# Streamed heads of a fused perceiver: the average's operands exchanged, one copy for the value blocks, and a turned quotient that VectorE copies behind its subtraction

## What is computed

```python
# _L0_ffn_ref: four expert attentions, x is (64, 32, 128), h = 16, hd = 8
q = (xg @ wq[e] + bq[e]).reshape(b, s, h, hd)
k = (xg @ wk[e] + bk[e]).reshape(b, s, h, hd)
v = (xg @ wv[e] + bv[e]).reshape(b, s, h, hd)
att = jnp.einsum('bqhd,bkhd->bhqk', q, k) * sm_scale
att = jax.nn.softmax(jnp.where(validg[:, None, None, :], att, -1e9), axis=-1)
y = jnp.einsum('bhqk,bkhd->bqhd', att, v).reshape(b, s, d)
y = y @ wo[e] + bo[e]
```

## Time and profile before

| | |
|---|---|
| median of 3 runs | 2164.21 us |
| lowest and highest run | 2162.43 and 2166.15 us |
| span of the profiled execution, first to last instruction | 2160.1 us |
| busy in the span: PE, DVE, ACT, POOL | 1764.0, 1435.0, 1016.2, 915.1 us |
| mean granted TensorE clock | 0.905 |
| the three streams: `L0Ffn`, `L1Attn`, `L3Ffn` | about 406 to 636, 718 to 779 and 1931 to 2023 us |

### The profile page before, as it was taken

One profiled execution on the slowest core, in us unless ns is written; L12 is line 12 of the kernel. 1 busy time (PEld: TensorE's weight loads), 2 busy tenths in 40 slices (PEclk: granted clock), 3 DMA queues, 4 the chain that ended last, 5 costly groups with the idle time before them and its releaser, 6 DMA issues.

```text
span 2160.1 us, 50856 instructions
## 1 busy us (share of the span) xinstructions
PE 1764.0 (82%) x20448; PEld 1176.2 (54%) x20448; DVE 1435.0 (66%) x3589; ACT 1016.2 (47%) x2574; POOL 915.1 (42%) x1083
## 2 busy tenths in 40 slices
PE   6678999899878789987578789998999896457496
PEld 4324557566544556643456656666676664135286
DVE  6799995688875665447970286565767666668622
ACT  5535764566644732242322365665666651124143
POOL 2243554455540514213522333137657567433433
PEclk9878999999999989999689999999999998757588
DMA  8000000100016100071033200100000000040187
GB/s 344 1 1 0 1 1 1 75 4 5 5 54 287 59 2 1 1 286 48 2 111 113 83 26 23 30 11 20 11 25 20 6 11 1 11 169 8 39 287 237
DMA packets 60427, 130.69 MB, mean 61 GB/s; under 512 B 16713, under 2 KB 38940, under 8 KB 54560
## 3 DMA queue, kind: packets, MB, share of 16 engines
q1 hardware_dynamic: 56896, 121.32, 15.7%
q0 software_dynamic: 3296, 6.12, 0.9%
HBM read 107.97 MB, written 20.12 MB: 59 GB/s over the span
## 4 chain that ended last, share of the span: by engine, by line
PE 48%; DVE 23%; issue 14%; ACT 7%; DMA 3%; SPq 2%; POOL 2%; POOLq 0%; DVEq 0%; ACTq 0%
PE PS L3230 4%; PE PS L2517 4%; PE PS L3277 3%; PE PS L424 3%; PE PS L3261 2%; PE PS L3219 2%; PE PS L3262 2%; DMA arena<-in_ctx 2%; PE PS L460 2%; DVE arena L1808 2%; PE PS L2317 2%; PE PS L4222 2%; PE PS L4231 1%; DVE arena L253 1%; PE PS L3269 1%
## 5 line engine op out<-in xcount | busy, mean ns | idle before, releaser
L321 POOL TENSOR_TENSOR arena<-arena 128x4 f32<-128x4 f32 (+3 forms) x109 | 118.7, 1090 | 396.5 <-DVE arena L264 260.0
L3345 ACT ACTIVATE arena<-PS,arena 128x289 f32<-128x289 f32 x256 | 128.0, 507 | 79.0 <-DVE arena L3459 78.1
L3230 PE MATMUL PS<-arena 128*128 128x289 f32 x512 | 153.4, 423 | 11.5 <-ACT arena L3345 7.5
L3459 DVE TENSOR_REDUCE arena<-PS 128x1 f32<-128x289 f32 x256 | 111.0, 453 | 75.2 <-PE PS L3230 70.0
L1872 POOL TENSOR_TENSOR arena<-arena 128x128 f32<-128x128 f32 x384 | 140.9, 405 | 43.1 <-PE PS L1735 18.9
L1258 POOL TENSOR_TENSOR arena<-arena 128x512 f32<-128x512 f32 x64 | 84.0, 1312 | 109.7 <-DVE arena L1403 109.7
L1808 DVE RECIPROCAL arena<-PS 128x128 f32<-128x128 f32 x96 | 91.6, 954 | 56.9 <-PE PS L1773 48.0
L1839 ACT COPY arena<-PS 32x128 f32<-32x128 f32 x384 | 99.7, 260 | 49.2 <-PE PS L1749 44.2
L3230 PEld LDWEIGHTS PS<-arena 128*128 128x128 f32 x512 | 87.9, 192 | 38.2 <-ACT arena L3345 19.6
L3188 POOL TENSOR_TENSOR arena<-arena 128x1024 f32<-128x1024 f32 x14 | 33.0, 2359 | 166.0 <-ACT arena L3336 166.0
L460 PE MATMUL PS<-arena 128*128 128x128 f32 (+4 forms) x576 | 84.9, 294 | 21.8 <-DVE arena L4338 7.8
(11 more groups left out here) (451 smaller groups left out, 4838.8 us busy)
## 6 DMA issues: line engine op xcount, KB each, us to landing
arena<-in_ctx SPq DMA_DIRECT2D x32, 1091.0 KB
arena<-in_f_w SPq DMA_DIRECT2D x39, 514.0 KB
arena<-in_ctx SPq DMA_DIRECT2D x16, 834.0 KB, 23.1
lists<-arena SPq DMA_DIRECT2D x8, 1040.0 KB, 10.6
arena<-in_f_w SPq DMA_DIRECT2D x32, 256.0 KB
arena<-in_ctx SPq DMA_DIRECT2D x16, 512.0 KB
arena<-in_mid SPq DMA_DIRECT2D x1, 3796.5 KB, 12.5
arena<-in_late SPq DMA_DIRECT2D x1, 3204.0 KB, 10.3
```

Source lines behind the costliest of these rows:

```text
L321: e.tensor_tensor(x, x, half.broadcast_to(list(x.shape)), ALU.pow).then_inc(*T.done("norm_root", tag))
L3230: e.matmul(PS[:, b, 0:UL], self.qt[i % 2][:, j, P * k:P * k + P], self.kt[i % 3][:, j, :], start=True, stop=True).then_inc(*T.done("k3_sco ...
L3345: e.activation(self.weights(n, k, 0, UL), PS[:, self.score_bank(n, k), 0:UL], ACT.Exp, bias=self.st[:, h, k:k + 1], accum_out=self.st[:, h ...
L3459: e.tensor_reduce(self.st[:, n % 2, k:k + 1], PS[:, self.score_bank(n, k), 0:UL], AXX, ALU.max, negate=True).then_inc(*T.done("k3_least", ...
```

## The change

- **values.** TensorE writes each head's values into their own columns of bank 4 (block j, group n, head h), so the bank holds the blocks as they are needed and zeros elsewhere; four matmuls against a cleared tile set these zeros once for each stream, ahead of the first scores. ACT takes the whole bank in one copy of 128x512.
- **vB** is 36 columns wide a block: 32 of values and four of ones (`rowmask`), written once by POOL in place of the memsets.
- **average.** Operands are exchanged: the turned weights are the PE weights now, the value blocks are streamed (16 matmuls of 36 columns). The result has the tokens on the partitions, with the sums of the weights beside it, so the four matmuls of L1773 go.
- **divide.** The reciprocal is taken of 128x16, and the product is written to a new tile `mean`.
- **back and out.** One transpose on PE turns `mean` into columns 256 to 383 of bank 7, and DVE copies that (128x128) to `OT`. Both come one step later than the division: `back(m - 3)` right behind the scores of m, `out(m - 3)` behind the subtraction of m (in `L1Attn` behind the causal product of m-1) and ahead of the division of m-2. `h_out`, for which the average of the next tile and the output projection wait, is now the end of that copy.

```diff
-    BANK = 5
+    BANK, WIDE = 5, S + HG
...
-        self.vB = [room.take(BT * D) for _ in range(3)]
+        self.vB = [room.take(BT * NG * self.WIDE) for _ in range(3)]
...
+            own = PS[:, 4, :].rearrange("p (j n h d) -> p j h n d", j=BT, n=NG, h=HG)
             for j in range(BT):
                 for h in range(HG):
-                    k = e.matmul(PS[S * h:S * h + S, 4, S * j:S * j + S].rearrange("p (n d) -> p n d", n=NG),
+                    k = e.matmul(own[S * h:S * h + S, j, h],
                                  self.xT[:, P * i + S * j:P * i + S * j + S], wv[:, h], start=True, stop=True)
...
-            for j in range(BT):
-                for n in range(NG):
-                    r = slice(S * n, S * n + S)
-                    k = e.matmul(PS[r, 7, S * j:S * j + S], v[:, D * j + S * n:D * j + S * n + S],
-                                 p[:, P * n + S * j:P * n + S * j + S], start=True, stop=True)
             for n in range(NG):
-                k = e.matmul(PS[S * n:S * n + S, 7, P:2 * P], g.C["headsum"], p[:, P * n:P * n + P], start=True, stop=True)
+                for j in range(BT):
+                    a = NG * j + n
+                    k = e.matmul(PS[S * j:S * j + S, 7, w_ * n:w_ * n + w_], p[:, P * n + S * j:P * n + S * j + S],
+                                 v[:, w_ * a:w_ * a + w_], start=True, stop=True)
             k.then_inc(*T.done("h_average", (tag, m)))
             free[7] = ("h_out", (tag, m))
+
+        def back(m):
+            for w in T.due(("h_mean", (tag, m))):
+                e.wait_ge(*w)
+            e.transpose(PS[:, 7, 2 * P:3 * P], self.mean[m % 2], g.C["ident"]).then_inc(*T.done("h_back", (tag, m)))
+
+        for w in T.due(free[4], ("h_cleared", tag)):
+            e.wait_ge(*w)
+        for j in range(BT):
+            e.matmul(PS[:, 4, P * j:P * j + P], self.mean[0], g.C["ident"], start=True, stop=True)
 
         for m in range(self.N + 3):
             if m < self.N:
                 scores(m)
+            if 0 <= m - 3 < self.N:
+                back(m - 3)
+            if m < self.N:
                 values(m)
...
-            e.reciprocal(rest, PS[:, 7, P:2 * P]).then_inc(*T.step())
-            for w in T.due(T.prev()):
-                e.wait_ge(*w)
-            e.tensor_tensor(self.OT[:, P * i:P * i + P], PS[:, 7, 0:P], rest, ALU.mult).then_inc(*T.done("h_out", (tag, m)))
+            e.reciprocal(rest.rearrange("p (n h) -> p n h", n=NG), both[:, :, S:]).then_inc(*T.step())
...
+            e.tensor_tensor(self.mean[m % 2].rearrange("p (n h d) -> p n h d", n=NG, h=HG),
+                            both[:, :, 0:S].rearrange("p n (h d) -> p n h d", h=HG),
+                            spread(rest.rearrange("p (n h) -> p n h", n=NG), [P, NG, HG, HD], 3),
+                            ALU.mult).then_inc(*T.done("h_mean", (tag, m)))
+
+        def out(m):
+            i = m % NT
+            for w in T.due(("h_back", (tag, m))):
+                e.wait_ge(*w)
+            e.tensor_copy(self.OT[:, P * i:P * i + P], PS[:, 7, 2 * P:3 * P]).then_inc(*T.done("h_out", (tag, m)))
...
+            if 0 <= m - 3 < self.N:
+                out(m - 3)
             if 0 <= m - 2 < self.N:
                 divide(m - 2)
             more(m)
...
-            for h in range(HG):
-                r = slice(S * h, S * h + S)
-                k = e.copy(v[r, :, h, :], PS[r, 4, 0:P].rearrange("p (a d) -> p a d", d=HD))
-            k.then_inc(*T.done("h_masked", (tag, m)))
+            e.copy(v, PS[:, 4, :].rearrange("p (a d) -> p a d", d=S)).then_inc(*T.done("h_masked", (tag, m)))
...
         for v in self.vB:
-            k = e.memset(v, 0.0)
-        k.then_inc(*T.done("h_cleared", tag))
+            v = v.rearrange("p (a w) -> p a w", w=self.WIDE)
+            e.tensor_copy(v[:, :, S:], spread(self.g.C["rowmask"], [P, BT * NG, HG], 1))
+        e.memset(self.mean[0], 0.0).then_inc(*T.done("h_cleared", tag))
```

More of the change, by code:

```diff
@@ L1708, in __init__ @@
         self.pT = [room.take(NG * P) for _ in range(2)]
-        self.vB = [room.take(BT * D) for _ in range(3)]
+        self.vB = [room.take(BT * NG * self.WIDE) for _ in range(3)]
         self.mx = [room.take(H) for _ in range(3)]
-        self.rest = [room.take(P) for _ in range(2)]
+        self.rest = [room.take(H) for _ in range(2)]
+        self.mean = [room.take(P) for _ in range(2)]
     def part(self, m):
@@ L1763, in average @@
         def average(m):
-            v, p = self.vB[m % 3], self.pT[m % 2]
+            v, p, w_ = self.vB[m % 3], self.pT[m % 2], self.WIDE
             for w in T.due(free[7], ("h_pT", (tag, m)), ("h_masked", (tag, m)), ("h_cleared", tag)):
                 e.wait_ge(*w)
-            for j in range(BT):
-                for n in range(NG):
-                    r = slice(S * n, S * n + S)
-                    k = e.matmul(PS[r, 7, S * j:S * j + S], v[:, D * j + S * n:D * j + S * n + S],
-                                 p[:, P * n + S * j:P * n + S * j + S], start=True, stop=True)
             for n in range(NG):
-                k = e.matmul(PS[S * n:S * n + S, 7, P:2 * P], g.C["headsum"], p[:, P * n:P * n + P], start=True, stop=True)
+                for j in range(BT):
+                    a = NG * j + n
+                    k = e.matmul(PS[S * j:S * j + S, 7, w_ * n:w_ * n + w_], p[:, P * n + S * j:P * n + S * j + S],
+                                 v[:, w_ * a:w_ * a + w_], start=True, stop=True)
             k.then_inc(*T.done("h_average", (tag, m)))
             free[7] = ("h_out", (tag, m))
+        def back(m):
[6 more added lines that the diff above has]
+            e.matmul(PS[:, 4, P * j:P * j + P], self.mean[0], g.C["ident"], start=True, stop=True)
         for m in range(self.N + 3):
@@ L1804, in divide @@
         def divide(m):
-            rest, i = self.rest[m % 2], m % NT
+            rest, both = self.rest[m % 2], PS[:, 7, 0:NG * self.WIDE].rearrange("p (n w) -> p n w", n=NG)
             for w in T.due(("h_average", (tag, m))):
                 e.wait_ge(*w)
-            e.reciprocal(rest, PS[:, 7, P:2 * P]).then_inc(*T.step())
-            for w in T.due(T.prev()):
+            e.reciprocal(rest.rearrange("p (n h) -> p n h", n=NG), both[:, :, S:]).then_inc(*T.step())
+            for w in T.due(T.prev(), ("h_back", (tag, m - 2))):
                 e.wait_ge(*w)
-            e.tensor_tensor(self.OT[:, P * i:P * i + P], PS[:, 7, 0:P], rest, ALU.mult).then_inc(*T.done("h_out", (tag, m)))
+            e.tensor_tensor(self.mean[m % 2].rearrange("p (n h d) -> p n h d", n=NG, h=HG),
[7 more added lines that the diff above has]
+            e.tensor_copy(self.OT[:, P * i:P * i + P], PS[:, 7, 2 * P:3 * P]).then_inc(*T.done("h_out", (tag, m)))
         def turned(m):
@@ L1833, in values @@
         def values(m):
-            v = self.vB[m % 3].rearrange("p (a h d) -> p a h d", h=HG, d=HD)
+            v = self.vB[m % 3].rearrange("p (a w) -> p a w", w=self.WIDE)[:, :, 0:S]
             for w in T.due(("h_values", (tag, m)), ("h_average", (tag, m - 3)), ("h_cleared", tag)):
                 e.wait_ge(*w)
-            for h in range(HG):
-                r = slice(S * h, S * h + S)
-                k = e.copy(v[r, :, h, :], PS[r, 4, 0:P].rearrange("p (a d) -> p a d", d=HD))
-            k.then_inc(*T.done("h_masked", (tag, m)))
+            e.copy(v, PS[:, 4, :].rearrange("p (a d) -> p a d", d=S)).then_inc(*T.done("h_masked", (tag, m)))
         for m in range(self.N + 3):
```

## The result

The changed kernel takes 2193.57 us in the median of four runs, the kernel before 2163.32: a ratio of 1.0151, 95% interval 1.0128 to 1.0174, some 30 us slower where +6.5 was forecast, and above the forecast's whole range (2158 to 2182). The profiled execution is the longest of the four; its span is 34.5 above that of the earlier trace rows.

A forecast was written before the change was run, and what follows sets the result against it. It took VectorE's 2.52 us loop to bound plain L0Ffn steps, TensorE's list those with projections. L0Ffn +0.5, L1Attn +4 and L3Ffn +2 summed to +6.5 on 2164.2: 2171 us, forecast 2166 to 2178, whole range 2158 to 2182.

The forecast's parts named there:

- The wait that it adds: Average waits for VectorE's copy behind the next subtraction, making a one-step loop: plain L0Ffn step 2.93 us, against 2.76.
- first 48 tiles: L0Ffn's three experts with projections: eight steps 27.24 us, 3.41 a step against 3.50, gaining 4.3 us.
- The transpose: On TensorE, 0.12 us in L0Ffn behind the full-shape mask; 0.22 in the other streams, with a change of shape.
- the prices of `L1Attn`: Loop of 3.39 us to the next average, output projections added: +4 us, between +2 (gaps covered) and +7 (none).
- Three steps add 0.99: In L1Attn, three steps each add an output projection of 0.99 us to the loop of 3.39.
- Last expert: L0Ffn's last 15 steps, without projections: lose up to 6 us, taken as 3.5, leaving out the next layer's norm.
- `L3Ffn`, +2 forecast: VectorE bounds L3Ffn; its order grows from 2.52 to 2.66 us plus layer work, 15 x 0.14 = 2.1.
- Zeroing and exit, 1.3: In L0Ffn, four zeroing matmuls ahead of the stream cost 1.0 us; the last tile's extra hand-over costs 0.3.
- The price of the average, 0.40: On TensorE, 36-column average to the next scores takes 0.40 us; bounds 0.28 and 0.46.
- The relief (1): Rival: copy ready by the turn's end, TensorE's list bounds L0Ffn; about -12 us, 2152; chance 0.10.
- The stall (3): Rival: VectorE's unexplained 8.82 us idle before L3Ffn's last reciprocal moves off; some 7 less, 2164; chance 0.08.
- Rival 4: TensorE's gaps lie inside loops without slack: L1Attn +7, L0Ffn +5, L3Ffn +4 us, 2180; chance 0.14.

The follow-up runs named there:

- copy_first: The changed kernel with VectorE's copy moved ahead of the subtraction, only VectorE's order changed: 2149.77 us, 0.9928 of the kernel before.
- before_late: The kernel before with the product in its own tile and VectorE copying it to OT a step later, behind the next subtraction: 2255.51 us, 1.0490.
- busy_l1: The changed kernel plus one unread matmul of 384 columns ahead of TensorE's wait in nine steps of L1Attn: 2187.78 us, 1.0112 of the kernel before.
- tail_early: The changed kernel with only each stream's last tile copied right behind its division: 2186.78 us, 1.0147 of the kernel before.
- values_only: The kernel before with only the value blocks' part of the change (whole bank 4, zeroing matmuls, one ScalarE copy): 2164.66 us, 1.0001.
- act_early: The changed kernel with the copy to OT on ScalarE, ahead of its copy of the values: 2123.56 us, 0.9861 of the kernel before.
- before_again: The kernel before, unchanged, run and profiled once more on another chip; the base there for the repeated runs, its own time not given.
- after_again: The changed kernel, unchanged, run once more on another chip: 2194.34 us, 1.0155 of the kernel before.
- act_early_again: act_early repeated with more rounds on another chip: 2142.26 us, 0.9910 of the kernel before.
- last_only: The changed kernel with ScalarE copying only every fourth tile, the one an output projection waits for: 2153.52 us, 1.0000 of the kernel before.
- busy_all: busy_l1 with the same unread matmul also in every step of L0Ffn's last expert and of L3Ffn: 2183.56 us, 1.0093 of the kernel before.

## Why the prediction was right in its sign and wrong in its size

**The wait that it adds: right.** "This decides" held; the place of the copy makes the change slower (copy_first: the same work with the copy moved ahead is at 0.993; before_late: the wait and its copy without the rest are at 1.049). In `L0Ffn` the loop was read closely: plain 2.96 (forecast 2.93), behind a bias add 3.30 (3.26), behind a projection copy 3.36 (3.32).

**Sizes off in the first 48 tiles (-4.3 forecast, +0.5 measured).** Projection steps take 3.27 (3.12), output projections 4.11 and 4.51 (3.92 and 4.31). For the output projections the timeline shows where the 0.2 is: the copy ends at 486.22, the output projection starts at 486.37 and the average at 487.43, 0.15 and 1.06 in place of 0.05 and 0.99.

```profile
485.94 0.28 DVE L1833 COPY arena<-PS 128x128 f32<-128x128 f32 x1
...
486.37 1.13 PE L460 MATMUL PS<-arena 128*128 128x128 f32 x8 [0.71 <-DVE arena L1833]
...
487.43 0.47 PE L1772 MATMUL PS<-arena 128*32 128x36 f32 x32
...
487.82 0.52 PE L1736 MATMUL PS<-arena 32*32 32x128 f32 x32
...
488.61 0.33 PE L1780 MATMUL PS<-arena 128*128 128x128 f32 x1
...
488.86 0.46 PE L1751 MATMUL PS<-arena 128*32 128x32 f32 x32
```

The transpose explains the projection steps, in which TensorE's own list decides. The forecast gave it 0.12, a quarter of the turn, since it "stands behind the mask, which has the full shape already". From its start to the values it takes 0.25 (488.61 to 488.86), about what it takes in `L1Attn` without a mask (0.26, 744.34 to 744.60). Eight steps are 28.1, not 27.24; times six, this is the miss. An output projection that follows a wait has to be priced from a start on an empty engine, and the earlier trace rows showed it behind other matmuls.

**The step that failed: the prices of `L1Attn`, "+4" for +11.5.** The forecast's loop of 3.39 was near (3.47), and it did add the three output projections ("Three steps add 0.99"). Twelve steps of 3.39, the three times 0.99 and three short first steps (7.8 as measured) are 51.5, its +2; for part of the gaps it went to +4, or 53.3. Measured were 60.8. Against the 51.5 two terms are missing (0.5 more lies in the loop itself and in the step of tile 3):
- *The clock.* The forecast has each group of matmuls at its duration in the kernel before. Behind waits of 1 to 2 us TensorE is seen at its lower level, where an output projection took 2.05 in place of 1.06 and a turn 1.12 in place of 0.66. The three steps with an output projection came to 17.9 in place of 3 x 4.38 = 13.1; with the clock up they were 4.57 each (busy_l1), so apart from the clock the three together cost 0.6 more than forecast. Tiles 12 and 13 took 4.50 and 4.27 in place of 3.48. In sum the clock is 5.5 in that profile, and 2.8 in tail_early's.
- *VectorE's work for the layer.* For `L0Ffn` the forecast had put the bias add into the loop; in `L1Attn` it left this work out. Tiles 7, 8 and 11, with bias add, copy or norm ahead of the causal product, took 4.10, 4.06 and 4.10, and the same with the clock up: 2.1 us.

**Last expert, +3.5 forecast, +5.7 measured.** "apart from the next layer's norm" left out what mattered: VectorE's norm work now stands inside the loop, ahead of the copy that an output projection waits for (6.38 and 6.04; 5.2 and 4.9 where the clock stayed up, busy_l1).

**`L3Ffn`, +2 forecast.** Steps +5.7, of which 4.0 in the steps with an output projection: the forecast has the average wait for VectorE's work there, but not the output projection. For the tail it had no term; it got +6.0, and in it the last copy stands behind 4 us of routing work:

```profile
2054.00 0.26 DVE L1821 RECIPROCAL arena<-PS 128x16 f32<-128x16 f32 x1 [9.66 <-remote]
2054.29 0.29 DVE L1824 TENSOR_TENSOR arena<-PS,arena 128x128 f32<-128x128 f32 x1
...
2058.37 0.28 DVE L1833 COPY arena<-PS 128x128 f32<-128x128 f32 x1
```

The product that was `h_out` before stood ahead of that work. tail_early shows about 2 of the tail by this. VectorE also has longer idle times there that nothing in its list ends: a new one of 3.35 stands ahead of the reciprocal at 2036.93, and all those over 2.5 us in the tail sum to 22.2 against 17.8 before (23.5 against 18.2 on the second chip). What causes them was not found, and how they and the copy's place share the tail's 6 is not shown.

**Zeroing and exit, 1.3:** smaller than the spread of the first column of the stage table; values_only is within 0.2% of before.

**The price of the average, 0.40:** 0.39 to 0.40 from its start to the scores (487.43 to 487.82). By the Trainium skill, TensorEngine Tiling (Array Packing), Instruction Overhead, a matmul of 1 column lasts as long as one of 60; with that, 36 columns would cost what 32 did, and the estimate would have been 0.37. This trace is nearer to the time growing with the columns, though 0.03 is little to decide by.

**The rivals.** The relief (1) does win once the wait is away: 0.991 and 0.986. The stall (3) stayed, 9.66 for the earlier trace rows's 8.82. Rival 4, the gaps add up, had the right direction for `L1Attn` (+7) and was still too low (2180): what came on top of the loop was the clock and VectorE's work, not TensorE's gaps.

## What to carry to other kernels

When a result gets a later last step, list every reader of it in every caller of the code, and price the rarest: here the steps of one tile in four held the whole loss against before. Then list what its engine does ahead of that step in each caller, since all of it gets into the loop. Place a short copy that others wait for ahead of the long work of its own engine, even where that engine then has to wait for it: 0.4 us of idle time on VectorE a step bought some 44 us, and on ScalarE (act_early) it bought as much or more (0.986 and 0.991 against 0.993). Where a loop gets new waits, look at the granted clock before adding up durations of the old trace.

Ask also whether each wait is needed. The output projection reads what the copy writes, but the average does not: it writes columns 0 to 143 of bank 7, which the product has read by then, and the copy reads columns 256 to 383. Its wait for `h_out` comes from `free[7]`, which stands for the whole bank. No run takes this wait away, so it is not shown what that would be worth, or whether both engines can work in one bank at that point.

## What the runs showed of the hardware

- VectorE's long idle times late in the program, which nothing in its list releases, were absent on one chip. before_again has 9.04 and 9.13, after_again 3.35, 2.73, 8.23 and 9.21, act_early_again 6.72 and 9.26, all on one chip; and every other profile but three has such times too. The three are act_early, last_only and before_late, all on one other chip: they have none above 0.5, though VectorE waits 4.0, 2.8 and 2.6 there ahead of the last reciprocal of `L3Ffn`, released by the average. The tail of act_early is 147.3 us there against 159.8. The kernel before is 0.5% faster on that chip as well (2150.9 against 2161.7); it was not profiled there.
- A matmul of 384 columns that nobody reads, ahead of TensorE's wait in 37 steps, made the changed kernel 11 us faster on one chip (busy_all against after_again, the four times of each apart). With it in nine steps of `L1Attn` alone (busy_l1) the layer was 5.5 us shorter in the profile, at a granted clock of 0.94 for 0.78; the ratios of the whole time, 1.0112 and 1.0151, overlap in their intervals.
- The lower level of the clock began at another tile in each of three executions of the same `L1Attn` code (6, 9 and 12).
- Four transposes take 0.66 at the full clock and 1.12 at the half; four float32 matmuls of an output projection 1.06 and 2.05.
